# Second routing of a two-layer kernel: five groups of batches in place of four, its sends begun in pass 5

## The reference, cut to what matters

```
x = x + s * g                       # end of layer 0, batch by batch
xn = _layernorm(x, axis=-1)
s = _L1_attn_ref(xn, ...)
g = _silu(_L1_ffn_ref(xn, ...))     # E, TOP_K, D, H = (8, 2, 128, 256)
...
logits = xt @ gate_w.T + gate_b
top_v, top_i = jax.lax.top_k(logits, TOP_K)
h0 = jnp.einsum('td,ehd->eth', xt, w0) + b0[:, None, :]
h1 = jnp.einsum('td,ehd->eth', xt, w1) + b1[:, None, :]
act = h0 * jax.nn.silu(h1)
out_all = jnp.einsum('eth,edh->etd', act, w2) + b2[:, None, :]
w = jax.nn.softmax(top_v, axis=-1)[:, :, None]
out = (w * sel).sum(axis=1)
```

## Time and profile before

| what | value |
|---|---|
| median of 3 runs | 1188.52 us (1180.65 to 1189.01) |
| the profiled execution's own time | 1175.42 us |
| its span, first to last instruction | 1173.5 us |
| PE, DVE, ACT, POOL busy | 86%, 67%, 55%, 49% of the span |
| pass 5 (routes 16 tiles) | 470.7 to 541.8 us |
| sends of the second routing | 542.0 to 803.2 us |
| second experts' first tile arrives | 808 us |

### The profile page before, as it was taken

How to read it: one execution, slowest core, us unless ns; L and a number is a source line. 1 busy time by engine, 2 the same in 40 slices (tenths; PEclk the granted TensorE clock), 3 DMA queues, 4 the chain that set the end, 5 groups by cost and what they waited for, 6 DMA issues and landing times.

```text
span 1173.5 us, 22918 instructions
## 1 busy us (share of the span) xinstructions
PE 1005.4 (86%) x7466; PEld 543.6 (46%) x7466; DVE 787.6 (67%) x2434; ACT 646.6 (55%) x1252; POOL 576.8 (49%) x670
## 2 busy tenths in 40 slices
PE   4757889998989898887988877777999899899888
PEld 2522269633333333332423444445888654444434
DVE  5597833488788887878777755674444587788741
ACT  1204732476767677665757643454444477667665
POOL 5266600155546373728678887741000264545564
PEclk8657989999999999999989988887999999999988
DMA  5852457662414050412323142234888544354221
GB/s 146 203 157 65 127 161 210 212 155 47 100 36 111 9 125 15 100 37 56 99 60 99 39 117 58 47 95 134 247 245 248 145 114 120 82 125 108 69 59 46
DMA packets 121864, 129.81 MB, mean 111 GB/s; under 512 B 13920, under 2 KB 104864, under 8 KB 121536
## 3 DMA queue, kind: packets, MB, share of 16 engines
q1 hardware_dynamic: 115184, 115.37, 37.9%
q0 software_dynamic: 6144, 12.60, 4.2%
q10 hardware_dynamic: 432, 0.52, 0.2%
HBM read 82.54 MB, written 52.35 MB: 115 GB/s over the span
## 4 chain that ended last, share of the span: by engine, by line
PE 56%; DVE 15%; issue 8%; POOL 7%; DMA 6%; ACT 4%; another core or an unknown queue 1%; SPq 1%; POOLq 0%; DVEq 0%; ACTq 0%
PE ps_banks L588 7%; PE ps_banks L629 7%; PE ps_banks L1810 5%; PE ps_banks L634 5%; DVE a_neg_max L888 4%; PE ps_banks L595 4%; DVE a_masked L894 3%; PE ps_banks L674 3%; PE ps_banks L1548 3%; PE ps_banks L1823 2%; PE ps_banks L1562 2%; PE ps_banks L726 2%; POOL sent L1673 2%; PE ps_banks L732 2%; PE ps_banks L640 2%
## 5 line engine op out<-in xcount | busy, mean ns | idle before, releaser
L777 ACT ACTIVATE a_probs<-ps_banks 128x512 f32<-128x512 f32 x512 | 278.9, 600 | 125.2 <-PE ps_banks L588 119.8
L588 PE MATMUL ps_banks<-q_strip,k_strip 53*128 53x512 bf16 (+3 forms) x1024 | 280.3, 352 | 67.5 <-DVE a_neg_max L888 24.4
L888 DVE TENSOR_REDUCE a_neg_max<-ps_banks 128x1 f32<-128x512 f32 x448 | 283.4, 682 | 63.8 <-PE ps_banks L595 57.2
L595 PE MATMUL ps_banks<-k_strip,q_strip 51*128 51x512 bf16 (+3 forms) x1024 | 289.2, 364 | 23.9 <-DVE a_neg_max L885 15.9
L894 DVE CUSTOM_DVE_ANT_0 a_masked<-ps_banks,mask_wide 128x384 bf16<-128x384 f32 (+3 forms) x512 | 223.8, 487 | 83.5 <-PE ps_banks L595 72.8
L779 ACT ACTIVATE a_probs<-ps_banks 128x512 f32<-128x512 f32 x256 | 144.5, 603 | 86.9 <-PE ps_banks L546 76.7
L1078 POOL DMA_INDIRECT tokens<-made,at x96 | 93.2, 971 | 178.1 <-DMA made<-work 126.0
L588 PEld LDWEIGHTS ps_banks<-q_strip,k_strip 53*128 53x128 bf16 x1024 | 72.6, 95 | 162.4 <-issue 60.3
L629 PE MATMUL ps_banks<-a_probs,v_aug 128*32 128x512 f32 x1024 | 139.7, 618 | 0.3
L595 PEld LDWEIGHTS ps_banks<-k_strip,q_strip 51*128 51x128 bf16 x1024 | 72.6, 95 | 131.3 <-ACT a_probs L777 62.4
L545 PE MATMUL ps_banks<-mask_kq,ident_halves 64*128 64x256 bf16 (+1 forms) x320 | 80.2, 261 | 0.3 <-issue 0.3
(11 more groups left out here) (259 smaller groups left out, 1753.2 us busy)
## 6 DMA issues: line engine op xcount, KB each, us to landing
work<-in_pack SPq DMA_DIRECT2D x39, 450.0 KB, 3.4
q_rows<-a_q_parts SPq DMA_DIRECT2D x96, 128.0 KB
k_rows<-a_k_parts SPq DMA_DIRECT2D x96, 128.0 KB
q_strip<-q_rows SPq DMA_DIRECT2D x64, 192.0 KB
k_strip<-k_rows SPq DMA_DIRECT2D x64, 192.0 KB
work<-in_w SPq DMA_DIRECT2D x32, 256.0 KB, 3.1
sent<-in_zeros SPq DMA_DIRECT2D x14, 512.0 KB, 8.0
work<-sent SPq DMA_DIRECT2D x55, 128.0 KB, 3.2
```

The source lines that it names most:

```text
L588: mm = pe.matmul(sbank[:, at:at + hi - lo], k_now[rows(js, ROW_END), slot, kt * P:(kt + 1) * P], q_now[rows(js, ROW_END), slot, lo:hi], st ...
L595: mm = pe.matmul(mbank[:, at:at + hi - lo], q_next[rows(jm, ROW_SHIFT), slot, qt * P:(qt + 1) * P], k_next[rows(jm, ROW_SHIFT), slot, lo:h ...
L777: act.activation(probs[si // 4 % 2][:, si % 4, :], bank, ACT.Exp).then_inc(sems["probs"], 1)
L888: dve.tensor_reduce(neg_max[:, half, qt, hd:hd + 1], bank, AX.X, ALU.max, negate=True).then_inc(sems["max_out"], 1)
```

## The change

Group 0 is cut in two: tiles 0 to 7 are routed in pass 4 and tiles 8 to 15 in pass 5. The other three groups keep their tiles, passes and places and only move up by one in number. The sends move:

| pass | tiles before (places) | tiles now (places) |
|---|---|---|
| 5 | none | 0 to 3 (0, 15) |
| 6 | 0 to 7 (0, 15, 19, 24) | 4 to 11 (0, 15, 19, 25) |
| 7 | 8 to 15 (0, 14, 18, 25) | 12 to 17 (0, 14, 25) |
| 8 | 16 to 23 (0, 7, 17, 23) | 18 to 23 (0, 7, 17) |
| 9 | 24 to 31 (4, 10, 18) | 24 to 31 (4, 10, 18) |

```diff
-GROUPS1 = ((0, 16), (16, 24), (24, 28), (28, NT))
+GROUPS1 = ((0, 8), (8, 16), (16, 24), (24, 28), (28, NT))
...
-    NB - 3: routed(0, (12, 14, 16, 18), 20, (22, 24, 25), 27, 29, 31),
+    NB - 4: routed(0, (12, 14, 16, 18), 20, (22, 24, 25), 27, 29, 31),
+    NB - 3: merged(routed(1, (12, 14, 16, 18), 20, (22, 24, 25), 27, 29, 31), sends(0, *2 * (0,), *2 * (15,))),
...
```

More of the change, by code:

```diff
@@ L201 @@
     2: {24: [("masks", 0)]},
-    NB - 3: routed(0, (12, 14, 16, 18), 20, (22, 24, 25), 27, 29, 31),
[L203 to L206, removed]
+    NB - 4: routed(0, (12, 14, 16, 18), 20, (22, 24, 25), 27, 29, 31),
+    NB - 3: merged(routed(1, (12, 14, 16, 18), 20, (22, 24, 25), 27, 29, 31), sends(0, *2 * (0,), *2 * (15,))),
+    NB - 2: sends(4, *2 * (0,), *2 * (15,), *2 * (19,), *2 * (25,)),
+    NB - 1: merged(routed(2, (12, 13, 15, 16), 18, (20, 21, 22), 23, 24, 26), sends(12, *2 * (0,), *2 * (14,), *2 * (25,))),
+    NB: merged(routed(3, (13, 14, 15, 16), 17, (20, 21, 22), 25, 26, 27), sends(18, *2 * (0,), *2 * (7,), *2 * (17,))),
+    ROUTE1: merged(routed(4, (8, 9, 10, 11), 13, (15, 16, 17), 18, 19, 21), sends(24, *2 * (4,), *2 * (10,)), sends(28, *4 * (18,))),
     **{MIX1 + i: mixed(-2, 8, 0, 18, 22, 24, 26, 28) for i in range(4)},
```

## The result

| | before | changed |
|---|---|---|
| median of 7 runs each, same chip | 1184.81 us (1179.03 to 1189.01) | 1196.4 us (1195.33 to 1207.12) |
| ratio, 95% interval | | 1.0115 [1.0084, 1.0146] |
| profiled execution's own time, span | 1175.42, 1173.5 us | 1207.12, 1205.2 us |

The time forecast was 1197.0 us, the time measured 1196.4. That the two meet within 0.6 us is luck. The forecast stood on a base of 1188.5 us, 3.7 above the median of the seven runs of before, and a difference of +8.2; the difference measured is 1196.4 - 1184.8 = +11.6 as the medians have it and +13.6 by the ratio. Two more measurements of the same kernel (experiments 5 and 12) gave +10.3 and +12.0. So the change costs about 12 us, and the sum was some 4 short; a base too high by 3.7 made up for it.

A forecast was written before the change was run, and what follows sets the result against it. DVE's small operations were taken to set the pace in routing passes, with POOL waited for in passes 6 to 8. 8.7 + 0.4 + 0.7 + 0 - 1.6 + 0 = +8.2 us on 1188.5 gave 1197 us, range 1185 to 1204.

The forecast's parts named there:

- Pass 4, +8.7 us: Pass 4: the added eight-tile routing costs its DVE operations' length, 9.5 less 0.8 us for narrower width; ends 0 and 9.5.
- Pass 5, +0.4 and +0.7: Pass 5: +0.4 us for six extra DVE operations less narrower width; +0.7 us for the added sends.
- four tiles of sends added, +0.7: Pass 5: sends at places 0 and 15 mostly covered by POOL's idle time; +0.7 us, ends 0 and 5.1.
- Pass 6, 0: Pass 6: same eight tiles' worth of sends at nearly the same places; 0, ends -0.5 and +0.5 us.
- Pass 7, -1.6: Pass 7: without place 18's sends the weighting ends before line 1943, whose comparison shortens; -1.6 us, ends 0 and -3.75.
- pass 8, 0: Pass 8: time freed at place 23 only lengthens POOL's wait for the moments; 0, ends 0 and -4.8 us.
- The slower rival: Pass 5: gate's weighting comes late, ACT waits at the tanh and the clock falls; +15.1 us, 1203.6 us; chance 0.20.
- The hidden routing: Pass 4: DVE's idle 11.5 us take up the added routing; -0.5 us in all, 1188 us; chance 0.09.
- the faster rivals: Passes 7 and 8: POOL's relief worth more, +1.3 us, chance 0.16; with the clock kept too, -7.8 us, chance 0.05.

The follow-up runs named there:

- experiment 5: The changed kernel measured again without edit, for a second profile: ratio to before 1.0087 [1.0051, 1.0123], +10.3 us.
- experiment 12: The changed kernel measured a third time without edit, for a third profile: ratio to before 1.0101 [1.0064, 1.0139], +12.0 us.
- experiment 1: Kernel before with the change's five routing groups but the sends left where they were: ratio to before 1.0089 [1.0058, 1.0120], +10.5 us.
- experiment 2: Changed kernel with tiles 0 to 3 never sent, so pass 5 routes but sends nothing: ratio to before 1.0113 [1.0076, 1.0150], +13.3 us.
- experiment 6: Kernel before with 14 DVE operations of the expert choice added in passes 3 and 4, results unused: ratio to before 1.0074 [1.0047, 1.0101], +8.7 us.
- experiment 3: Kernel before with tiles 12, 13, 22 and 23 (passes 7 and 8) never sent: ratio to before 0.9967 [0.9941, 0.9993], -3.9 us.
- experiment 4: Kernel before with one pair of sends in each of passes 6 and 7 moved to place 30: ratio to before 1.0099 [1.0060, 1.0138], +11.7 us.
- experiment 7: Kernel before with tiles 4 and 5 (pass 6, place 19) never sent: ratio to before 0.9945 [0.9918, 0.9973], -6.5 us.
- experiment 9: Kernel before with one pair of sends moved from pass 6 to pass 9: ratio to before 0.9989 [0.9964, 1.0014].
- experiment 10: Kernel before with two pairs of sends, from passes 6 and 7, moved to pass 9: ratio to before 0.9971 [0.9952, 0.9991], -3.3 us.
- experiment 11: Changed kernel with three pairs of sends in pass 6 instead of four, later sends shifted: ratio to before 1.0017 [0.9990, 1.0043].
- experiment 8: Kernel before with groups of 12, 12, 4, 4 tiles, no routing in pass 5, sends from pass 5 on: ratio to before 0.9968 [0.9936, 1.0000].

## Why the prediction was right and where it was not

The time and the main cost were right, one routing more in pass 4. The sum fell short in pass 5, where one term had the wrong mechanism, and in pass 4 in those executions in which the clock fell; a base that was too high hid both.

*Pass 4, +8.7 us: the mechanism was right.* +8.3 in the first profile, +8.8 and +8.2 in experiments 1 and 2. Experiment 6 shows for the 14 operations of the choice, some 4.3 of the 7.1 us of DVE, that they cost what they last; for the tile ends, the weights and the count on PE and ACT it is argued from pass 5, not taken apart. What the term lacked is the second form, 12.1 and 12.4 us in experiments 5 and 12. It was outside the term's own ends, 0 and 9.5: the clock of pass 5 in one profile was taken as the clock that such a pass gets.

*Pass 5, +0.4 and +0.7: mis-sized.* It took +7.7, +3.4 and +3.1 us in three profiles; the pass 5 of before itself lasts 71.0 to 73.3 us in seven profiles (before and experiments 3, 4, 6, 7, 9, 10). Pass 5 of before in three stretches, up to the moments of line 1011, to the tanh, to the end:

```profile
470.70:488.70 18.00, 17.03 (x117) 7.42 (x116) 14.57 (x45) 13.04 (x25) 11.46 (x15) 1.00 0.63 139
488.70:523.00 34.30, 28.99 (x202) 13.03 (x200) 27.68 (x61) 21.48 (x43) 16.02 (x23) 1.00 0.20 44
523.00:541.80 18.80, 13.64 (x78) 3.83 (x74) 17.31 (x42) 10.31 (x20) 13.07 (x21) 0.82 0.01 2
```

The changed kernel in the same stretches, first profile:

```profile
478.10:499.20 21.10, 18.08 (x116) 7.74 (x114) 14.10 (x44) 13.02 (x25) 15.55 (x18) 0.92 0.53 130
499.20:536.60 37.40, 33.22 (x202) 13.69 (x200) 26.51 (x62) 21.43 (x43) 19.12 (x26) 0.86 0.20 48
536.60:556.90 20.30, 14.53 (x78) 3.62 (x74) 18.43 (x47) 10.14 (x20) 13.43 (x23) 0.74 0.00 1
```

And experiment 5:

```profile
482.60:502.20 19.60, 17.80 (x118) 7.64 (x117) 14.81 (x46) 13.01 (x25) 15.42 (x18) 1.00 0.55 131
502.20:537.00 34.80, 30.26 (x202) 12.95 (x200) 26.57 (x62) 21.37 (x43) 19.08 (x26) 0.95 0.24 57
537.00:557.10 20.10, 14.43 (x86) 3.97 (x82) 17.61 (x47) 11.62 (x24) 13.29 (x23) 0.83 0.01 2
```

The front stretch is 3.1 and 1.6 us longer (experiment 12: 1.4; experiment 11, with the same sends: 0.4). Without sends at place 0 it lasts 17.9 to 18.0 us in the seven profiles just named, and 17.4 and 17.6 in experiments 1 and 2. Two rows of before at the pass's start, POOL and DVE; then the same DVE operation and POOL's wait for the moments in the first profile; then both in experiment 11:

```profile
472.48 0.23 POOL L1011 TENSOR_SCALAR a_ln3a_veps<-a_ln3a_moments 128x4 f32<-128x4 f32 x1 [1.79 <-DVE a_ln3a_moments L855]
475.31 0.26 DVE L921 RECIPROCAL a_o_den<-ps_banks 128x16 f32<-128x16 f32 x1 [0.56 <-PE ps_banks L640]
```

```profile
484.32 0.26 DVE L922 RECIPROCAL a_o_den<-ps_banks 128x16 f32<-128x16 f32 x1 [2.62 <-remote]
499.21 0.26 POOL L1012 TENSOR_SCALAR a_pmom_veps<-a_pmom_moments 128x8 f32<-128x8 f32 x1 [3.04 <-DVE a_pmom_moments L856]
```

```profile
483.86 0.26 DVE L922 RECIPROCAL a_o_den<-ps_banks 128x16 f32<-128x16 f32 x1 [0.61 <-PE ps_banks L641]
497.23 0.26 POOL L1012 TENSOR_SCALAR a_pmom_veps<-a_pmom_moments 128x8 f32<-128x8 f32 x1 [1.26 <-DVE a_pmom_moments L856]
```

The failed step is the term "four tiles of sends added, +0.7", and it failed in its mechanism. I let the 3.06 us wait swallow what it could of the 5.1 us and carried the other 2.0 along POOL's list to the scan. But POOL already idles 1.79, 0.89 and 0.18 us before that wait, at the normalisation and the splits; these 2.9 us go first, 2.2 come off the wait, and about 0.8 of it would be left. In POOL's own list the four sends are covered whole: in experiment 11 POOL waits 1.26 us, with a front stretch 0.4 longer. What makes the front longer is not on POOL. About 6 us into the pass DVE stands at the reciprocal of line 922, and ACT beside it, although PE's product is done: 2.62 us in the first profile, 1.43 and 1.50 in experiments 5 and 12, 1.04 in experiment 8, 0.61 in experiment 11. In passes 3 to 5 and in all 14 profiles that wait is 0.37 to 0.61 us wherever no sends stand at place 0 (37 passes); in pass 6, where they always do, it is 1.13 to 1.99 in eight profiles and 0.37 to 0.41 in six. So sends at a pass's start go with a stop of DVE and ACT of up to 2 us that some executions have and others do not; the mechanism is not shown. In experiments 5 and 12 it makes up some 0.9 of the 1.6 and 1.4 us; in the first profile 2.1 of the 3.1, and a low clock stands behind it (the products of line 675 take 2.08 us, 1.13 in experiment 5). A delay of DVE and PE is not covered by POOL's idle time in front of the scan, and it stays in the pass.

The last stretch is 1.3 to 1.5 us longer, in experiments 1, 2 and 11 too (20.5, 20.3 and 20.2): the second group's six extra operations stand there, and the clock differs; the term for both, with the narrower width, was +0.4. The middle is nearly even in experiment 5 (+0.5 at a clock of 0.95); its 3.1 us in the first profile come at a clock of 0.86 against 1.00. So of the +3.1 to +3.4 us, some 1.5 are sends and the rest the split and its clock. Of the first profile's further 4.4, 1.5 lie in front, where the clock is 0.92, and 2.7 in the middle. Experiment 2 warns against reading more out of it: with no sends in the pass it took 74.2 us too, its middle 36.3 at a clock of 0.91 (tanh at 527.20). The sends and a turn of the clock look alike in the length of one pass; only the front stretch tells them apart.

*Pass 6, 0:* held roughly, +1.1, +1.0, +0.6 us, just at the bound of 1; with the same eight tiles' sends the pass lasts 68.1 to 71.3 us in experiments 1 to 3 and 6, so a bound of 1 us could not tell anything.

*Pass 7, -1.6, and pass 8, 0:* by rows the relief came where it was said; by length the two passes together changed by +3.1, -0.7 and -0.1 us against before's profile, the first of these at a clock of 0.74 in pass 8. But that profile (136.4 us for the two) is the shortest of the four with all sends kept there: experiments 1, 6 and 7 have 138.4, 140.5 and 138.7. Against experiment 1, which has the change's routing, experiments 2, 5 and 12 are 2.8, 2.7 and 2.1 us shorter, so the forecast's -1.6 is rather small than large. The weighting found another DVE operation to slow, and POOL's time was given back as waits of 3.85 and 9.22 us. The step as forecast was also read too simply: line 1943 began at 655.07, 0.69 us before the weighting (655.76) and while POOL's fourth send was under way, so the weighting alone did not hold it up. Alone, the relief was worth 3.9 [0.8, 6.9] (experiment 3).

*The slower rival* gave nearly the right size (+15.1) with the wrong mechanism: no wait at the tanh. *The hidden routing* (-0.5) and *the faster rivals* fell. The pass lengths of experiments 5 and 12 exceed before's by 15.8 and 16.0 us, 7.7 more than the sum: 3.6 in pass 4, 2.1 in pass 5, 0.8 in pass 6 and 1.2 in passes 7 and 8. The totals show 4 of these 7.7; the profile of before is itself a short one, in passes 7 and 8 (above) and as a whole (1175.42 us against a median of 1184.8). The totals of the same kernel differ by about as much (+13.6, +10.3, +12.0), so no finer account can be made.

## What to carry to other kernels

Before work is split in more groups, count how much of its price goes with its width and how much with the number of its operations: here eight tiles cost 8 to 9 us (12 in the executions where the clock fell) and sixteen cost 9.5, so every further group is paid nearly in full on an engine that looks one fifth idle. When work is put on an engine with idle time, add up all its waits from there on, not the longest alone, and then look at the other engines at the same moment: here POOL had room for the sends, and the time was lost on DVE and ACT. And look for relief where another engine is seen waiting in the middle of a pass (pass 6, 5 to 6 us for one pair), not where the busy share is highest (passes 7 and 8, 3.9 us for two pairs).

## What the runs showed of the hardware that was not expected

- The same instruction list in the same pass took either 69.8 to 70.4 or 73.7 to 74.0 us, by whether the granted clock dropped once (late in the pass, 0.79 over its last 16.6 us) or already from its middle on (0.73). A single profile of such a pass can be 4 us off.
- A short DVE TENSOR_TENSOR on SBUF that begins beside a POOL TENSOR_TENSOR of 1 us or more mostly ends only with it: in the 14 traces, 203 of 226 that usually last under 0.35 us and began with over 0.15 us of POOL's operation left. DVE, then POOL, in pass 3 of experiment 6:

```profile
369.33 1.30 DVE L1149 TENSOR_TENSOR work<-work,consts 128x64 f32<-128x64 f32 x1
...
377.23 0.22 DVE L1149 TENSOR_TENSOR work<-work,consts 128x64 f32<-128x64 f32 x1
```

```profile
369.30 1.26 POOL L1054 TENSOR_TENSOR work<-work,be 128x512 f32<-128x512 f32 x1
```

The first comparison ends at 370.63, the layer norm's operation at 370.56; its twin, with POOL idle, takes 0.22. The 0.98 us of pass 7 after (ends at 667.95, the weighting at 667.93) is the same. The 1.83 us of pass 7 before ends with the weighting too (656.90 and 656.81) but begins before it, beside a send:

```profile
654.77 0.97 POOL L2011 DMA_INDIRECT sent<-xn,at  x1 [0.30 <-issue]
```

Moving POOL's operation only changed which DVE operation was hit. It is not every pair: beside POOL's TENSOR_SCALAR the operation of DVE ended first in the changed kernel (757.24 against 757.84).

```profile
756.77 0.47 DVE L1951 TENSOR_TENSOR m_past<-consts,work 1x312 f32<-1x312 f32 x1
756.63 1.21 POOL L1058 TENSOR_SCALAR work<-work,a_fmom_moments,a_fmom_rstd 128x128 f32<-128x128 f32 x1
```

- Sends at the start of a pass go with a stop of DVE and ACT of up to 2 us at the step of line 922, in 12 of the 19 passes that have them and in none of the 37 that have not.
